# A four-layer graph kernel: the decay masks of layer 2 counted in the first sweep, one triangle matmul a tile, two evictions a chunk on VectorE

## The reference, cut to what matters

```python
# layer 0
Ax = A @ x;  out = 1 - 0.1 * x - 0.01 * sum(x * Ax, axis=1)
# layer 1, twice
x = tanh(concat([adj @ x, x]) @ W[k])
# layer 2: only the last 100 neighbours of a row count, with halving weights
support = input @ weight
mask = (adj != 0)
rank = cumsum(mask, axis=1); deg = rank[:, -1:]
k = minimum(deg, 100); pos = rank - (deg - k)
w = mask * where(pos > 0, 0.5 ** (k - pos), 0)
out = w @ support + bias
# layer 3
h = tanh(concat([X, t]) @ W1 + b1)
out = h @ W2 + b2 + Wt @ XB - sum(Wt, axis=1) * XB
```

## Time and profile before

| | us |
|---|---|
| median of three runs | 831.64 |
| the profiled execution | 832.51 |
| its span, first to last instruction | 830.7 |
| busy: TensorE 739.1, VectorE 445.3, ScalarE 200.5, GpSimd 126.3 | |

### The profile page before, as it was taken

How to read it: one execution, slowest core, us unless ns; L and a number is a source line. 1 busy time by engine, 2 the same in 40 slices (tenths; PEclk the granted TensorE clock), 3 DMA queues, 4 the chain that set the end, 5 groups by cost and what they waited for, 6 DMA issues and landing times.

```text
span 830.7 us, 10008 instructions
## 1 busy us (share of the span) xinstructions
PE 739.1 (89%) x3717; PEld 293.7 (35%) x3736; DVE 445.3 (54%) x765; ACT 200.5 (24%) x287; POOL 126.3 (15%) x148
## 2 busy tenths in 40 slices
PE   3877878889999999999999798889888979999998
PEld 1222222223433344444444243334333433343333
DVE  5111111147666676767667788888888852111110
ACT  2000000000100000100001576566656640211111
POOL 5001111110000001221112201101110113322221
PEclk9999999999999999999999899999999999999999
DMA  9999999999999999999899666667666747999995
GB/s 375 416 420 419 421 420 421 419 375 376 398 389 389 388 385 346 342 359 334 336 361 362 223 226 221 241 222 266 216 246 221 266 165 277 349 348 368 374 360 208
DMA packets 45984, 275.16 MB, mean 331 GB/s; under 512 B 5104, under 2 KB 13424, under 8 KB 13552
## 3 DMA queue, kind: packets, MB, share of 16 engines
q1 hardware_dynamic: 36720, 266.13, 83.0%
q10 hardware_dynamic: 9216, 8.39, 3.0%
HBM read 270.31 MB, written 4.19 MB: 330 GB/s over the span
## 4 chain that ended last, share of the span: by engine, by line
PE 44%; DMA 27%; DVE 22%; issue 4%; POOL 2%; ACT 1%; DVEq 1%; POOLq 0%
PE accA L922 31%; DMA land<-adj_blocks 26%; DVE uS L757 16%; PE tr L822 2%; PE spare L934 2%; PE spare L937 2%; PE nat L846 1%; PE nat L842 1%; PE accA L947 1%; POOL rstd L434 1%; PE spare L877 1%; DVE uS L740 1%; DVE st L626 1%; PE nat L838 1%; DMA xin<-x_rows 1%
## 5 line engine op out<-in xcount | busy, mean ns | idle before, releaser
L922 PE MATMUL accA<-land,X 128*64 128x512 f32 x1504 | 352.5, 598 | 23.1 <-DMA land<-adj_blocks 21.9
L922 PEld LDWEIGHTS accA<-land,X 128*64 128x64 f32 x1504 | 100.7, 136 | 214.4 <-issue 144.5
L582 ACT ACTIVATE wS<-spare 128x1024 uint16<-128x1024 f32 x128 | 131.0, 1024 | 86.7 <-PE spare L937 84.1
L922 PE MATMUL accA<-cache,X 128*64 128x512 f32 x544 | 131.9, 605 | 22.1 <-DVE X L787 12.6
L757 DVE SCALAR_TENSOR_TENSOR uS<-land,uS 128x512 bf16<-128x512 f32 x180 | 128.5, 714 | 19.7 <-DVE uS L757 0.5
L934 PE MATMUL spare<-uS,triA 128*128 128x512 bf16 x248 | 94.7, 386 | 31.2 <-DVE uS L757 28.4
L441 POOL TENSOR_TENSOR hS<-tS 128x256 f32<-128x256 f32 x32 | 25.7, 805 | 561.8 <-DVE tS L627 561.8
L937 PE MATMUL spare<-uS,triB 128*128 128x512 bf16 x246 | 94.3, 383 | 0.5 <-ACT wS L582 0.2
L740 DVE TENSOR_TENSOR wS<-wS,land 128x512 f32<-128x512 f32 x96 | 66.8, 695 | 39.4 <-DMA land<-adj_blocks 36.8
L740 DVE TENSOR_TENSOR uS<-uS,land 128x512 f32<-128x512 f32 x92 | 64.6, 702 | 32.4 <-DMA land<-adj_blocks 29.6
L947 PE MATMUL accA<-wS,X 128*128 128x512 bf16 x247 | 74.5, 381 | 0.3
(11 more groups left out here) (76 smaller groups left out, 436.2 us busy)
## 6 DMA issues: line engine op xcount, KB each, us to landing
land<-adj_blocks SPq DMA_DIRECT2D x235, 1024.0 KB, 7.6
cache<-adj_blocks SPq DMA_DIRECT2D x17, 1024.0 KB, 12.8
xin<-x_rows ACTq DMA_DIRECT2D x32, 128.0 KB, 6.2
x_rows<-zS ACTq DMA_DIRECT2D x24, 128.0 KB, 4.7
cache<-x_rows SPq DMA_DIRECT2D x1, 1024.0 KB, 4.9
out_rows<-zS ACTq DMA_DIRECT2D x8, 128.0 KB, 7.0
wts<-weights SPq DMA_DIRECT2D x1, 675.0 KB, 6.2
cache<-triangles SPq DMA_DIRECT2D x1, 128.0 KB, 6.0
```

Source lines behind the costliest of these rows:

```text
L582: nc.scalar.activation(weights(c, b).bitcast(U16), spare[:, 2 * k:2 * k + 2, :].rearrange("p a b -> p (a b)"), ACT.Relu)\
L922: last = nc.tensor.matmul(accA[k * D:(k + 1) * D, c % 2, :], tile(X[p % 2], TQ * b + k), of[:, k * W:(k + 1) * W], start=(b == 0), stop=(b ...
```

## The change

- L2 runs forward. VectorE makes one plain mask a block, 1024 wide (`tensor_scalar`, not_equal, float32 to bfloat16), on 127 of the 128 partitions; no running sum. The ring holds 8 blocks.
- The number of nonzeros in all later tiles comes in on partition 127 of the mask, by DMA. So one triangle a tile does: `triB` is gone, and a block has four matmuls instead of six.
- These numbers are made in L0: VectorE makes the mask of every block there too, and TensorE multiplies it with a 128 x 64 stationary of ones (`count`, two bfloat16 matmuls a block, on the two halves of the array's columns as in the sweep) into `spare`. At the end of a chunk ScalarE copies one half, VectorE adds the other, and ScalarE stores 64 KB to DRAM (`counts_d`).
- In L2, SyncE issues a small load a pair (`counts_for`: 4 rows of 1 KB onto partition 127), and nine small loads a chunk (`left_over`: row 127 of each tile, and its counts).
- The neighbours on partition 127 itself are weighed apart: GpSimd makes their weights for a chunk in three instructions on 32 x 512, and TensorE adds one matmul a chunk. Once, SyncE copies their rows of `support` out to DRAM and back and waits for the first half of that.
- VectorE instead of ScalarE evicts blocks 4 and 12 of each chunk, issued behind the masks of blocks 7 and 15.
- A landing slot of L0 is free when block and mask are done; before L2's first loads, SyncE waits for the last sums of L1B (`sums_done`).
- The totals all lie in `uS`. 16 pairs are cached instead of 17, so every sweep behind L0 loads one more (chunk 0, pair 1).
- The order in chunk 0 with `HELD` is gone; the blocks are weighed in order.

The core of the diff:

```diff
-    return (0, 1, 4) if c == 0 else (0, 4)
+    return (0, 4)
...
-LOADS = [(p, c, k) for p in range(5) for c in range(NC) for k in pair_order(p) if (c, 2 * k) not in CACHE_SLOT]
+LOADS = [(p, c, k) for p in range(5) for c in range(NC) for k in range(PAIRS) if (c, 2 * k) not in CACHE_SLOT]
...
+MASKS = 8
+AHEAD = 3
 WRING = 4
-def weigh_order(c):
-    pairs = list(range(NQ))
-    return pairs[HELD:14] + pairs[:HELD] + pairs[14:] if c == 0 else pairs
-def weigh_no(c, pair):
-    return NQ * c + weigh_order(c).index(pair)
-def weight_slot(c, pair):
-    if c == 0 and pair < HELD:
-        return WRING + pair
-    return (NQ * c + pair - HELD) % WRING
-def weight_before(c, pair):
-    g = NQ * c + pair - WRING
-    return (g // NQ, g % NQ) if g >= HELD else None
+EVAC_DVE = (4, 12)
+EVAC_LAG = 3
+LAST = P - 1
...
-        uS = sb("uS", [P, 8 * W], BF16)
-        wS = sb("wS", [P, (WRING + HELD) * 2 * W], F16)
+        uS = sb("uS", [P, MASKS * BLK], BF16)
+        wS = sb("wS", [P, WRING * BLK], F16)
         wts = sb("wts", [P, NCOLS], F32)
         triA = sb("triA", [P, P], BF16)
-        triB = sb("triB", [P, P], BF16)
+        later = sb("later", [P, 4 * NT], BF16)
+        loS = sb("loS", [NT, P], F16)
+        loadjS = sb("loadjS", [NT, W], F32)
+        locntS = sb("locntS", [NT, W], BF16)
+        lowS = sb("lowS", [NT, 2 * W], U16)
...
+        def weights_out(eng, ops, c, b):
+            n = NQ * c + b
+            eng.wait_ge(tri_done, n + 1)
+            if n >= WRING:
+                eng.wait_ge(w_used, n - WRING + 1)
+            k = b % 2
+            w, of = weights(n).bitcast(U16), spare[:, 2 * k:2 * k + 2, :].rearrange("p a b -> p (a b)")
+            if b in EVAC_DVE:
+                ops.tensor_scalar(w, of, 0.0, None, ALU.max).then_inc(w_ready_dve, 1)
+            else:
+                ops.activation(w, of, ACT.Relu).then_inc(w_ready, 1)
...
+            def counts_for(g):
+                if g < MASKS // 2:
+                    sp.wait_ge(sums_done, 2 * g + 2)
+                else:
+                    sp.wait_ge(tri_done, 2 * (g - MASKS // 2) + 2)
+                c, k = g // PAIRS, g % PAIRS
+                at = (2 * k) % MASKS * BLK
+                sp.dma_start(uS[LAST:P, at:at + 2 * BLK].rearrange("o (t w) -> o t w", w=W),
+                             tile_counts[c, 4 * k:4 * k + 4, 0].rearrange("(o t) w -> o t w", o=1))\
+                    .then_inc(counts_in[g % (MASKS // 2)], 16)
+            def left_over(c):
+                if c:
+                    sp.wait_ge(left_ready, c)
+                rows = adj_in.rearrange("(b p) (t w) -> p b t w", p=P, t=2 * TQ)
+                for k in range(PAIRS):
+                    sp.dma_start(loadjS[4 * k:4 * k + 4, :], rows[LAST, c * PAIRS + k]).then_inc(left_in, 16)
+                sp.dma_start(locntS[:, :], tile_counts[c, :, 1]).then_inc(left_in, 16)
+            def after_masks(g):
+                for i in range(counts_to[0], min(g + AHEAD, PAIRS * NC - 1) + 1):
+                    counts_for(i)
+                    counts_to[0] = i + 1
+                if g % PAIRS == 3 and g // PAIRS + 1 < NC:
+                    left_over(g // PAIRS + 1)
+                if g == 6:
+                    sp.wait_ge(copy_used, copied_no(L1B, NC - 1, 1) + 1)
+                    sp.dma_start(left_d, X[1][LAST:P, :].bitcast(F16)).then_inc(left_rows, 16)
+                    sp.wait_ge(left_rows, 16)
+                    sp.dma_start(loS[:, :], left_d.rearrange("o (t w) -> (o t) w", w=2 * D)).then_inc(left_rows, 16)
+            counts_to = [0]
...
+                if p == L2 and c == 0:
+                    sp.wait_ge(counts_out, 16 * NC)
+                    left_over(0)
+                    after_masks(0)
...
                         pp, pc, pk = LOADS[n - LAND]
-                        if pp == L2:
-                            sp.wait_ge(u_ready, NT * pc + 2 * (NQ - 1 - 2 * pk) + 2)
-                        else:
+                        if pp != L2:
                             sp.wait_ge(swept, sweep_no(pp, pc, 2 * pk + 1) + 1)
+                        if pp in (L0, L2):
+                            sp.wait_ge(u_ready, mask_no(pp, pc, 2 * pk + 1) + 1)
                         for pq in (2 * pk, 2 * pk + 1):
                             if totals_block(pp, pq):
                                 sp.wait_ge(totalled, totalled_no(pp, pc, pq))
                     sp.dma_start(land[:, n % LAND, :], rows).then_inc(landed[n % LAND], 16)
+                    if n >= LAND and pp == L2:
+                        after_masks(PAIRS * pc + pk)
...
+            def left_over(c):
+                w = left_weights(c)
+                pool.wait_ge(left_in, 16 * (PAIRS + 1) * (c + 1))
+                if c >= 2:
+                    pool.wait_ge(weighed, c - 1)
+                nc.gpsimd.tensor_scalar(loadjS[:, :], loadjS[:, :], 0.0, -NEIGH * BIT, ALU.is_equal, ALU.mult)\
+                    .then_inc(left_step, 1)
+                pool.wait_ge(left_step, 2 * c + 1)
+                nc.gpsimd.tensor_tensor(loadjS[:, :], loadjS[:, :], locntS[:, :], ALU.subtract).then_inc(left_step, 1)
+                pool.wait_ge(left_step, 2 * c + 2)
+                nc.gpsimd.tensor_scalar(w, loadjS[:, :], NEIGH * BIT, 0.0, ALU.add, ALU.max).then_inc(left_ready, 1)
...
+                if p == L0 and at == 4:
+                    act.wait_ge(counted, NQ * (c + 1))
+                    if c:
+                        act.wait_ge(count_ready, c)
+                    nc.scalar.activation(upperS, spare[D:P, c % 2, :], ACT.Copy).then_inc(count_half, 1)
+                if p == L0 and at == 7:
+                    act.wait_ge(count_ready, c + 1)
+                    act.dma_start(counts_d[c], countS).then_inc(counts_out, 16)
...
+                        dve.wait_ge(count_half, c + 1)
+                        if c:
+                            dve.wait_ge(counts_out, 16 * c)
+                        nc.vector.tensor_tensor(countS, upperS, spare[0:D, c % 2, :], ALU.add).then_inc(count_ready, 1)
...
-                if p == L2:
-                    q = NQ - 1 - b
-                    wait_landed(dve, p, c, q)
-                    for i in range(TQ):
-                        t = TQ * b + i
-                        k = TQ - 1 - i
-                        u = uS[:, (t % 8) * W:(t % 8 + 1) * W]
-                        of = block_of(p, c, q)[:, k * W:(k + 1) * W]
-                        if t >= 8 or c:
-                            dve.wait_ge(tri_done, NQ * c + (t - 7) // 2 + 1)
-                        if t == 0:
-                            nc.vector.tensor_scalar(u, of, 0.0, None, ALU.not_equal).then_inc(u_ready, 1)
-                        else:
-                            earlier = uS[:, ((t - 1) % 8) * W:((t - 1) % 8 + 1) * W]
-                            dve.wait_ge(u_ready, NT * c + t)
-                            nc.vector.scalar_tensor_tensor(out=u, in0=of, scalar=0.0, in1=earlier,
-                                                           op0=ALU.not_equal, op1=ALU.add).then_inc(u_ready, 1)
+                if p in (L0, L2):
+                    n = NQ * c + b
+                    wait_landed(dve, p, c, b)
+                    if n >= MASKS:
+                        dve.wait_ge(counted if p == L0 else tri_done, n - MASKS + 1)
+                    elif p == L2:
+                        dve.wait_ge(sums_done, b + 1)
+                    rows = P if p == L0 else LAST
+                    nc.vector.tensor_scalar(masks(b)[0:rows, :], block_of(p, c, b)[0:rows, :], 0.0, None, ALU.not_equal)\
+                        .then_inc(u_ready, 1)
+                if p == L2 and b - EVAC_LAG in EVAC_DVE:
+                    weights_out(dve, nc.vector, c, b - EVAC_LAG)
...
-            def triangle(c, pair):
-                pe.wait_ge(u_ready, NT * c + 2 * pair + 2)
-                if pair >= 2 or c:
-                    pe.wait_ge(w_ready, NQ * c + pair - 1)
-                for i in range(2):
-                    t = 2 * pair + i
-                    o = spare[:, 2 * (pair % 2) + i, :]
-                    last = nc.tensor.matmul(o, triA[:, :], uS[:, (t % 8) * W:(t % 8 + 1) * W],
-                                            start=True, stop=(t == 0))
-                    if t:
-                        last = nc.tensor.matmul(o, triB[:, :], uS[:, ((t - 1) % 8) * W:((t - 1) % 8 + 1) * W],
-                                                start=False, stop=True)
+                if p == L0 and b:
+                    count(c, b - 1)
+                elif p == L0 and c:
+                    count(c - 1, NQ - 1)
+            def count(c, b):
+                pe.wait_ge(u_ready, mask_no(L0, c, b) + 1)
+                if b == 0 and c >= 2:
+                    pe.wait_ge(count_ready, c - 1)
+                for k in range(TQ):
+                    t = TQ * b + k
+                    last = nc.tensor.matmul(spare[k * D:(k + 1) * D, c % 2, :], later[:, 2 * (NT - t):2 * (2 * NT - t)],
```

(46 more changed lines are left out.)

87 lines of the change are left out of this document (47 added, 40 removed).

## The result

The changed kernel takes 796.15 us, the median of four runs (794.82 to 797.59), beside 831.21 for the one before (830.36 to 833.84). The ratio is 0.9573, 95% interval 0.9545 to 0.9602: 35 us less. Forecast were 771, in a range of 748 to 806.

A forecast was written before the change was run, and what follows sets the result against it. Each sweep had its own limit: loads in L0, TensorE in L1A and L3, VectorE in L2. From 832.5 us, L2 gave -68.0, L0 +5, additional loads +2.5: 772.0, against the median 771, range 748 to 806.

The forecast's parts named there:

- GpSimd beside the masks: L2: VectorE loses 0 to 4.9 us a chunk to GpSimd's five data-moving instructions; 2.5 taken, giving 18.7.
- the rival of the full lock: L2: each of five GpSimd instructions stops VectorE for its whole length; chunk 21.9 us, time 791; chance 0.17.
- the rule of whole lengths: L2: such VectorE and GpSimd instructions exclude each other fully, the power included; 6.1 us a chunk, chunk 23.1, time 801.
- (a) to (c): L2: new waits for evictions behind masks, late count loads and the nine left_over issues; 0.8 us a chunk together.
- (d): L2's start: loads held until L1B's last sums, plus the wait for support rows; +5 us in place of 8.5.
- My sum of 19.5: L2's chunk period in us: VectorE's work of 18.7 plus 0.8 for new waits; 16.9 to 23.7 by its ends.
- (a): L2: evictions of blocks 4 and 12 stand behind masks on VectorE, and TensorE's triangles wait; within the shared 0.8 us.
- (c): L2: nine left_over issues a chunk delay the loads and counts behind them; up to 0.43 us each, 3.9 in all.
- L0, +5: L0: count matmuls side by side stay covered by loads; store 1.3, dry queue 2, coupled slots 1.7 us; together +5.
- The load more: One more load in each of L1A, L1B, L2 and L3; outside L2 between 0 and 7.5 us, 2.5 taken.
- Counts behind SyncE's loads (806): L2: 4.2 us for late counts and left_over issues paid in full every chunk; chunk 23.7, time 806; chance 0.10.
- The slower cases: L2's pairs wait for counts (889, chance 0.05; slower from a 10.1 us landing), or masks run at 1.26 us (852, 0.03).

The follow-up runs named there:

- the best kernel: Changed kernel with rows of x early, L2's loads first, L0's first-chunk counts held back, all evictions on ScalarE and count loads issued by ScalarE: 767.89 us.
- e11_rows_and_counts: Changed kernel with rows of x loaded early and counts issued by ScalarE, evictions of blocks 4 and 12 still on VectorE: 786.85 us, ratio 0.9459.

## Why the prediction was right or wrong

- **The stage and the sign.** L2 was VectorE's and no longer is; it gives 45.7 us, L0 takes 8.5 of them back and the other stages come to nothing, which is the 37.2 of the spans. Right.
- **The durations.** A mask takes 0.70 where GpSimd is idle (0.69 to 0.70 in L0), as worked out from L753 and L645. An eviction on VectorE takes 1.22 against 1.25. TensorE's 17.2 a chunk is close to what the best kernel comes to (busy 17.0 of 17.57). The count matmuls run side by side. Right. Not right is to add masks up by their durations: back to back they start 0.60 apart (six in 3.69 us), so sixteen are 9.7 and not 11.2. I had taken the running sums from start to start, but not the masks.
- **GpSimd beside the masks: 2.5 a chunk taken, 1.6 measured.** The three new instructions take 2.41, 1.20 and 2.54 us, 6.1 together, well over my bound of 3.7: on 32 partitions a one-input instruction cost twice L487 on 128. VectorE loses little of it. Two masks from 597.45 on take the usual 1.28 though the first of the three runs on GpSimd from 596.77 to 599.18; two from 599.79 on, beside the other two, take 2.20. So this instruction of GpSimd did not hold VectorE up for its whole length; the rival of the full lock was wrong, and where the rule of whole lengths that the prediction gives beside it says otherwise, the measurement decides. More important, the term did not belong on the path: with GpSimd's work cut, the time did not fall.
- **The new waits, "I take 0.8 for (a) to (c)": the step that failed, with (d).** My sum of 19.5 is VectorE's work, 18.7, plus this term. In the six chunks from 498.86 to 626.47 VectorE is busy 100.79 of 127.61 us, 16.8 a chunk (in the seventh it has made part of the masks ahead and has fewer left), and 4.5 of 21.3 are idle, so the measured period is no sum of one engine's work. That the period missed by only 1.5 is luck in part: VectorE's work was 1.9 too high in the sum and the waits nearly 4 too low. The low end of the range, 16.9, even lay below the 17.2 that I had for TensorE. (a) alone was more than what I gave to all three: TensorE stands 9.0 us in seven chunks for evictions on VectorE, 1.3 a chunk. (c), the nine issues, took 3.3 us of SyncE's time (3.9 was the bound). And the wait with the largest share of the chain was not in the list: the rows of x. The load is not new; its cover, 10.8 us from issue to use, was what the change halved. I had asked what hides each edit, not what each remaining transfer was hidden by.
- **(d), the start of L2, +5: 15.1.** L1B ends 9.8 us later than before (462.76 against 452.99), so the 461 forecast for the first load answers to 470.9 - 9.8 = 461.1: it came when forecast. Missed were the copy of the sums behind mask 2, for which the first triangle waits, and the clock of 0.76 in the chunk. The experiment that lifts it gains 6 us.
- **L0, +5: +8.5.** The dry queue was foreseen at 2 us from the slots alone, and with the counts held back the load does go out at 22.93, as forecast. TensorE's own wait for mask 0 came on top, 2 to 4 us by experiment. Store and coupled slots had 3.0 in the sum; from the second chunk on L0 lost 1.6 (20.90 against 20.64 a chunk), and which of the two it was isn't shown.
- **The load more, 2.5: 0.0.** L1A lost 1.9, L1B and L3 got it back.
- **The rivals.** Counts behind SyncE's loads (806) are real, but as the third of three waits: 8.5 us, seen clearly only when the two others were gone. The slower cases did not come; in the chains of the changed kernel and of the one with the rows early, counts take 5.2 to 7.0 us, under the 10.1 that would have decided. The Trainium skill, DMA: Bandwidth & Descriptors, "Queues, rings and completion order", has descriptors of a ring taken in order; the gain from moving the counts to ScalarE's queue fits, yet it also takes them from behind SyncE's waits, and no run separates the two.

## What to carry to other kernels

When a change speeds up the engine that sets a loop, every transfer and every small wait in that loop has less time to hide in, by the ratio of the periods: go through what is left, not only through what is edited. In-order queues turn such a wait into a stop of unrelated work, here masks behind the rows of x, sums behind a mask, an eviction behind a layernorm. Where several waits share one loop, test the fixes together too: one of them cost 7 us alone and gave 8.5 with the others.

## What the runs showed of the hardware that was not expected

- GpSimd's `tensor_scalar` on 32 x 512 with two operations takes 1.9 us alone and up to 2.54 beside VectorE, while `tensor_tensor` takes 1.22 on 128 x 512 and 1.14 to 1.2 on 32 x 512: for the latter the partitions hardly mattered, and the kind of instruction mattered more than either.
- Back to back, VectorE's masks start 0.60 us apart, though the profile shows 0.69 for each.
- Some stops of TensorE in L2 were followed by matmuls at 1.06 us a pair instead of 0.59 for about 3 us, and some of the same length were not. In the changed kernel the clock fell behind stops of 1.96, 2.03 and 2.54 us and not behind three of 1.68; with the rows of x early it fell behind three of four of 1.68; in `e11_rows_and_counts` it fell behind none of seven of 1.68 to 2.09. What decides isn't shown. Of the seven chunks after the first, the three in which it fell have a mean clock of 0.92, the others 1.00. There a stop cost more than itself: about 3.2 us at half speed do 1.6 us of work, an estimated 1.6 us lost.
